# Mixture-of-experts block: results added in memory by the scatter, and a last stage that reads four rows a token

## The reference

```python
    x = layernorm(x + conv_attention(x))
    x = layernorm(x + attention_mlp(x))
    x = layernorm(x + linear_attention(x))
    # 64 experts of width 176, six of them for each token
    topk_w, topk_idx = jax.lax.top_k(softmax(x @ gate_w.T), 6)
    topk_w = topk_w / jnp.sum(topk_w, axis=-1, keepdims=True)
    h = jax.nn.silu(jnp.einsum('th,eih->tei', x, experts_w1))
    y = jnp.einsum('tei,ehi->teh', h, experts_w2)
    routed_out = sum over the six experts e of y[t, e] * topk_w[t, e]
    x = layernorm(x + routed_out + shared_out)
```

## Time and profile before

| | us |
|---|---|
| median of 3 runs | 1036.09 (1034.62 to 1038.6) |
| span of the profiled execution | 1034.5 |
| TensorE busy in it | 967.6 (94%) |
| VectorE busy | 608.1 (59%) |
| GpSimd busy | 456.8 (44%) |
| ScalarE busy | 338.7 (33%) |

### The profile page before, as it was taken

How to read it: one execution, slowest core, us unless ns; L and a number is a source line. 1 busy time by engine, 2 the same in 40 slices (tenths; PEclk the granted TensorE clock), 3 DMA queues, 4 the chain that set the end, 5 groups by cost and what they waited for, 6 DMA issues and landing times. The chain is left out here.

```text
span 1034.5 us, 20988 instructions
## 1 busy us (share of the span) xinstructions
PE 967.6 (94%) x6481; PEld 799.2 (77%) x6481; DVE 608.1 (59%) x2176; ACT 338.7 (33%) x1038; POOL 456.8 (44%) x516
## 2 busy tenths in 40 slices
PE   7988999999999999999999899868999999999986
PEld 6766887877877877877887677647888888888865
DVE  4745466676676676666676546644555555555266
ACT  1244263264264264263263362101111111111243
POOL 1132152283283283283283371541566656656622
PEclk9999999999999999999999999888999999999999
DMA  9597790510510510510510510159869697878296
GB/s 360 192 277 136 203 263 10 133 38 23 137 37 21 137 37 21 137 38 20 128 43 17 129 52 11 64 211 317 335 205 351 211 311 232 295 229 304 85 347 219
DMA packets 103271, 163.28 MB, mean 158 GB/s; under 512 B 26961, under 2 KB 77106, under 8 KB 101042
## 3 DMA queue, kind: packets, MB, share of 16 engines
q1 hardware_dynamic: 85746, 113.31, 37.9%
q0 software_dynamic: 12288, 33.96, 8.7%
q10 hardware_dynamic: 5184, 15.36, 4.1%
HBM read 139.32 MB, written 61.87 MB: 194 GB/s over the span
## 5 line engine op out<-in xcount | busy, mean ns | idle before, releaser
L1282 ACT ACTIVATE prob<-bank,nmx 128x128 f32<-128x128 f32 (+1 forms) x256 | 104.9, 432 | 63.5 <-DVE nmx L1587 63.4
L641 POOL TENSOR_TENSOR prob<-prob,rec 128x512 f32<-128x512 f32 x96 | 99.3, 1041 | 40.8 <-DVE rec L1593 40.0
L673 POOL DMA_INDIRECT x_rows<-x_copy,desti x84 | 85.8, 1021 | 18.3 <-issue 18.3
L1587 DVE TENSOR_REDUCE nmx<-bank 128x2 f32<-128x512 f32 (+1 forms) x96 | 65.1, 685 | 46.6 <-PE bank L889 45.9
L1275 ACT ACTIVATE probT<-bank 128x512 f32<-128x512 f32 x96 | 58.0, 604 | 56.6 <-PE bank L749 55.8
L749 PE MATMUL bank<-cst,prob 128*128 128x128 f32 x384 | 60.6, 282 | 10.3 <-POOL prob L641 6.0
L663 POOL TENSOR_TENSOR products<-z,products 128x512 bf16<-128x512 f32 x8 | 9.2, 1155 | 136.6 <-ACT products L1263 136.6
L949 PE MATMUL bank<-h2T,w_up 128*128 128x256 f32 x256 | 66.4, 382 | 0.0
L951 PE MATMUL bank<-h2T,w_in 128*128 128x256 f32 x256 | 65.7, 379 | 0.0
L749 PEld LDWEIGHTS bank<-cst,prob 128*128 128x128 f32 x384 | 44.4, 145 | 20.2 <-POOL prob L641 10.1
L1282 ACT ACTIVATION_READ_ACCUMULATOR prob<-bank,nmx 128x1 f32 x256 | 55.8, 218 | 0.0
(11 more groups left out here) (445 smaller groups left out, 2500.9 us busy)
## 6 DMA issues: line engine op xcount, KB each, us to landing
w_in<-in_e_w SPq DMA_DIRECT2D x20, 448.0 KB
w_up<-in_e_w SPq DMA_DIRECT2D x20, 448.0 KB
w_down<-in_e_w SPq DMA_DIRECT2D x20, 448.0 KB
products<-in_e_w SPq DMA_DIRECT2D x20, 448.0 KB
prob<-in_e_w SPq DMA_DIRECT2D x20, 448.0 KB
probT<-in_e_w SPq DMA_DIRECT2D x20, 448.0 KB
actT<-in_e_w SPq DMA_DIRECT2D x20, 448.0 KB
x_rows<-sgt SPq DMA_DIRECT2D x1, 8320.0 KB, 28.9
```

Of the source, the lines that this page charges most:

```text
L641: pool.tensor_tensor(p, p, r, ALU.mult).then_inc(S["b_scaled"], 1)
L673: pool.indirect_dma_start(x_rows, bass.IndirectOffsetOnAxis(ap=desti[:, n:n + 1].bitcast(U32), axis=0), rows[:, n // TOPK, :], None).then_ ...
L1282: i = act.activation(prob[:, u % PROBS, h * w:(h + 1) * w], psum(u % 2, h * w, (h + 1) * w), ACT.Exp, bias=nmx[:, u, h:h + 1], accum_out=s ...
L1587: dve.tensor_reduce(nmx[:, u, 0:512 // w], bank[:, u % 2, :].rearrange("p (h k) -> p h k", k=w), AX, ALU.max, negate=True).then_inc(S["b_m ...
```

## The change

- `y_rows` becomes four accumulators: each token has four rows, and chunk n of a quad (n = 0 to 3) adds to row n. The indirect DMA gets `compute_op=ALU.add`. 8704 rows in place of 20608.
- Because an addition needs what is there, SyncE fills `y_rows` with zeros, out of the same `zeros` tile, behind the second fill of `x_rows`; `r_fill` is waited for at 80 in place of 64.
- Each scatter has an `alone` of its own, and waits until the scatter into the same accumulator of the quad before has landed.
- The weights travel with the row: meta data grow from 8 to 14 numbers, `TOPW` goes. `places` finds the weight of the row (`share`), and `result` multiplies by it on the way out of PSUM, four operations of 256 columns in place of two copies of 512.
- In the last turn the weights are worked out per half batch (`E4w`), ahead of `E5p`.
- The last stage loads four rows a token (512 KB) and has eight tiles in flight. TensorE adds them with the plain identity. VectorE adds the residual and takes the statistics; GpSimd does the power and one product; the scaling is an activation on ScalarE, with four output buffers.

```diff
+ACCS = 4
+XW = D + 2 + 2 * TOPK
+Y_ROWS = ACCS * (NB * L + P)
...
-YG = 4
+YG = 8
+OUTS = 4
...
-    c[:, 261:261 + TT] = (np.arange(TT) * P + p[:, None]) * TOPK
+    c[:, 261:261 + TT] = (np.arange(TT) * P + p[:, None]) * ACCS
...
-    blank[:, :, 0] = PAIRS + np.arange((E_N + SPARE + 1) * P).reshape(-1, P)
+    blank[:, :, 0] = ACCS * (NB * L + p)
...
-        outb = [t[:, 0, :] for t in ring(YG, P, 1, D)]
-        yg = [t[:].rearrange("p a b -> p (a b)")[:, 0:TOPK * D].rearrange("p (k d) -> p k d", k=TOPK) for t in (w_in, w_up, actT)]
-        yg.append(products[:].rearrange("p n f d -> p (n f) d")[:, 0:TOPK, :])
-        ON_PE = TOPK - 1
-        diag = [stack[n][:].rearrange("p h k l -> p (h k l)").bitcast(F32)[:, t * ON_PE * P:(t + 1) * ON_PE * P]
-                .rearrange("p (k c) -> p k c", k=ON_PE) for n in "qk" for t in range(2)]
-        ids, choice, found = sb("ids", [P, STREAMS], I32), sb("choice", [P, STREAMS]), sb("found", [P, 4, TOPK])
+        yg = [t[:].rearrange("p a b -> p (a b)")[:, h * ACCS * D:(h + 1) * ACCS * D].rearrange("p (k d) -> p k d", k=ACCS)
+              for h in range(2) for t in (w_in, w_up, w_down, actT)]
+        outb = [stack["k"][:].rearrange("p h k l -> p (h k l)").bitcast(F32)[:, t * D:(t + 1) * D] for t in range(OUTS)]
+        f_rows = stack["q"][:].rearrange("p h k l -> p (h k l)").bitcast(F32)[:, 0:OUTS * D].rearrange("p (t d) -> p t d", t=OUTS)
+        f_st, f_mv = sb("f_st", [P, OUTS, 6]), sb("f_mv", [P, OUTS, 2])
+        f_var, f_root, f_low, f_off = (sb(n, [P, OUTS]) for n in ("f_var", "f_root", "f_low", "f_off"))
+        ids, share, found = sb("ids", [P, STREAMS], I32), sb("share", [P, STREAMS]), sb("found", [P, 4, TOPK])
...
-                "dve": """E2v_0 E2w_0 E3n_0 E2v_1 E3o_0 E2w_1 E3n_1 E4m_0 E3o_1 E4t_0 E4k_0 E4m_1 E5p_0 E4t_1 E4k_1 E5h_0 E5p_1 DTa DTb E5h_1 DTe S0 S1 S2 D4w SD""",
+                "dve": """E2v_0 E2w_0 E3n_0 E2v_1 E3o_0 E2w_1 E3n_1 E4m_0 E3o_1 E4t_0 E4k_0 E4m_1 E4w_0 E5p_0 E4t_1 E4k_1 E4w_1 E5h_0 E5p_1 DTa DTb E5h_1 DTe S0 S1 S2 SD""",
...
             blank(x_rows[E_N * CAP:].rearrange("(n p) d -> p n d", p=P), E_N, SPARE + 1)
+            sp.dma_start(y_rows.rearrange("(n p) d -> p n d", p=P), zeros[:].rearrange("p (o d) -> p o d", o=1).broadcast_to([P, Y_ROWS // P, D])
+                         ).then_inc(S["r_fill"], 16)
             with sp.Fori(2, NB - 1) as b:
                 stack_up(b)
             stack_up(NB - 1)
-            sp.wait_ge(S["r_fill"], 64)
+            sp.wait_ge(S["r_fill"], 80)
...
             def spread(c):
-                need(pool, "p_spare", c.no + NB + 1)
                 pool.wait_ge(S["m_ids"], c.no + 1)
                 late = isinstance(c.no, int) and c.no >= QUADS - 2
                 pool.wait_ge(S["m_y_out"], 2 * c.no + (1 if late else 2))
-                alone(pool)
-                for k in range(4):
+                for k in range(ACCS):
                     if late and k == 2:
                         pool.wait_ge(S["m_y_out"], 2 * c.no + 2)
+                    need(pool, "p_spare", c.no * ACCS + k + NB + 1)
+                    need(pool, f"m_st{k}", c.no * 16)
+                    alone(pool)
                     s, n = 2 * c.slot(2) + k // 2, 4 * c.slot(RING) + k
-                    pool.indirect_dma_start(y_rows, bass.IndirectOffsetOnAxis(ap=ids[:, n:n + 1].bitcast(U32), axis=0), yc[s][:, k % 2, :], None
-                                            ).then_inc(S[f"m_st{s}"], 16)
+                    pool.indirect_dma_start(y_rows, bass.IndirectOffsetOnAxis(ap=ids[:, n:n + 1].bitcast(U32), axis=0), yc[s][:, k % 2, :], None,
+                                            compute_op=ALU.add).then_inc(S[f"m_st{k}"], 16)
             quad_loop(pool, [None, None, spread])
             def root(c):
-                h = c.slot(2)
+                at = slice(c.slot(OUTS), c.slot(OUTS) + 1)
                 pool.wait_ge(S["n_varF"], c.no + 1)
-                pool.tensor_tensor(nrm["F"]["y"][:, h:h + 1], nrm["F"]["v"][:, h:h + 1], minus_half[:, 0:1], ALU.pow
-                                   ).then_inc(S["n_invF"], 1)
+                pool.tensor_tensor(f_root[:, at], f_var[:, at], minus_half[:, 0:1], ALU.pow).then_inc(S["n_invF"], 1)
+                pool.wait_ge(S["n_invF"], c.no + 1)
+                pool.tensor_tensor(f_off[:, at], f_low[:, at], f_root[:, at], ALU.mult).then_inc(S["f_off"], 1)
             tile_loop(pool, [root])
...
                 pe.wait_ge(S[f"f_ld{s}"], c.before(YG) * 16 + 16)
-                pe.wait_ge(S["f_diag"], c.no + 1)
                 need(pe, "f_r", c.no - (YG - 1))
-                for k in range(ON_PE):
-                    mm = pe.matmul(psum(s, 0, D), diag[s][:, k, :], yg[s][:, k, :], start=(k == 0), stop=(k == ON_PE - 1))
+                for k in range(ACCS):
+                    mm = pe.matmul(psum(s, 0, D), ident, yg[s][:, k, :], start=(k == 0), stop=(k == ACCS - 1))
...
                     if n == 0 and first(b):
-                        act.wait_ge(S["r_fill"], 64)
+                        act.wait_ge(S["r_fill"], 80)
                     need(act, "d_sact", b * 3 + n)
...
-                rows = (slice(c.no * P * TOPK, (c.no + 1) * P * TOPK) if isinstance(c.no, int)
-                        else bass.ds(c.no * P * TOPK, P * TOPK))
-                act.dma_start(yg[s], y_rows[rows, :].rearrange("(p k) d -> p k d", k=TOPK)).then_inc(S[f"f_ld{s}"], 16)
-                if not isinstance(c.no, int):
-                    weigh(c)
-            def weigh(c):
-                w = tile_of(TOPW, c.no)
-                for k in range(ON_PE):
-                    i = act.activation(diag[c.slot(YG)][:, k, :], ident, ACT.Identity, scale=w[:, k:k + 1])
-                i.then_inc(S["f_diag"], 1)
+                rows = (slice(c.no * P * ACCS, (c.no + 1) * P * ACCS) if isinstance(c.no, int)
+                        else bass.ds(c.no * P * ACCS, P * ACCS))
+                act.dma_start(yg[s], y_rows[rows, :].rearrange("(p k) d -> p k d", k=ACCS)).then_inc(S[f"f_ld{s}"], 16)
...
             def put(c):
-                h = c.slot(2)
+                h = c.slot(OUTS)
+                at = slice(h, h + 1)
+                act.wait_ge(S["f_off"], c.no + 1)
+                need(act, f"f_st{h}", c.before(OUTS) * 16)
+                act.activation(outb[h], f_rows[:, h, :], ACT.Identity, scale=f_root[:, at], bias=f_off[:, at]).then_inc(S["f_out"], 1)
                 act.wait_ge(S["f_out"], c.no + 1)
                 n = slice(c.no, c.no + 1) if isinstance(c.no, int) else bass.ds(c.no, 1)
                 act.dma_start(out[n].rearrange("o p d -> p (o d)"), outb[h]).then_inc(S[f"f_st{h}"], 16)
-            act.wait_ge(S["d_dest"], NB + TT - 1)
-            for n in range(YG):
-                weigh(Tile(0, n))
-            for s in range(4):
-                act.wait_ge(S[f"m_st{s}"], 32 * (QUADS // 2))
-            tile_loop(act, [collect, None, None, None, put])
-            for h in range(2):
-                act.wait_ge(S[f"f_st{h}"], 16 * (NT // 2))
+            for k in range(ACCS):
+                act.wait_ge(S[f"m_st{k}"], 16 * QUADS)
+            tile_loop(act, [collect, *(YG - 1) * [None], put])
+            for h in range(OUTS):
+                act.wait_ge(S[f"f_st{h}"], 16 * (NT // OUTS))
...
             def D4w(b):
+                need(dve, "d_copied", b)
                 cd.link(dve.tensor_reduce(wsum[:], top8[:, :, 0:TOPK], AX, ALU.add))
                 cd.link(dve.reciprocal(wrec[:], wsum[:]))
-                cd.step(dve.tensor_tensor(slots(TOPW, b), top8[:, :, 0:TOPK],
+                cd.step(dve.tensor_tensor(x3_meta[:, :, 1 + TOPK:1 + 2 * TOPK], top8[:, :, 0:TOPK],
                                           wrec[:].rearrange("p (t o) -> p t o", o=1).broadcast_to([P, TT, TOPK]), ALU.mult))
+            def E4w(tt):
+                def part(b):
+                    need(dve, "d_copied", b)
+                    cd.link(dve.tensor_reduce(wsum[:, tt:tt + 1], top8[:, tt, 0:TOPK], AX, ALU.add))
+                    cd.link(dve.reciprocal(wrec[:, tt:tt + 1], wsum[:, tt:tt + 1]))
+                    cd.step(dve.tensor_scalar(x3_meta[:, tt, 1 + TOPK:1 + 2 * TOPK], top8[:, tt, 0:TOPK], wrec[:, tt:tt + 1], None, ALU.mult))
+                return part
...
-                for j in range(2):
-                    need(dve, f"m_st{2 * c.slot(2) + j}", c.before(2) * 32 - 32)
+                for k in range(ACCS):
+                    need(dve, f"m_st{k}", (c.no - (RING - 1)) * 16)
                 for n in range(4):
                     at, s = 4 * c.no + n, 4 * c.slot(RING) + n
                     meta = xc_row[s][:, D:XW]
                     e = expert_of[:, at:at + 1] if isinstance(c.no, int) else expert_of[:, bass.ds(at, 1)]
-                    i = dve.scalar_tensor_tensor(found[:, n, :], meta[:, 1:1 + TOPK], e, iota[:, 0:TOPK], ALU.is_equal, ALU.mult,
-                                                 accum_out=choice[:, s:s + 1])
```

(50 more changed lines are left out.)

4 lines of the change are left out of this document (2 added, 2 removed).

## The result

| | before | changed |
|---|---|---|
| median of the runs, us | 1035.99 | 1121.86 (1119.78 to 1125.41) |
| span of the profiled execution | 1034.5 | 1123.4 |
| up to the first `S0` | 157.06 | 201.49 |
| from there to the first scatter of results | 560.7 | 560.6 |
| first scatter of results to the landing of the last | 263.2 | 320.7 |

The changed kernel is slower: ratio 1.081, 95% interval 1.078 to 1.0845. The forecast was 1054 with a range of 1038 to 1090. The table accounts for all 88.9 us of span: +44.4 at the start, +57.5 in the expert loop, -13.0 in the last stage, and nothing in between. The profiled execution of the changed kernel took 1125.41 us and is the slowest of the four; the medians are 85.9 us apart.

A forecast was written before the change was run, and what follows sets the result against it. TensorE was taken as busy nearly everywhere, bounding the expert loop at 6.67 us a quad. Span 1034.5 + 25 + 1.5 + 0.3 + 1.3 + 3 - 13 = 1052.6; the median, 1.6 above, gives 1054 us, range 1038 to 1090.

The forecast's parts named there:

- (a): Start: the zero fill of `y_rows` queues ahead of ScalarE's first `sgt` write, landing at 182; +25 us (+15 to +30).
- Rivals C and D: Start: C, new fill runs beside tiny packets, 1038 us, chance 0.09; D, ScalarE's wait isn't reached, 1028 us, chance 0.06.
- (b): After TensorE's stand at the start: a few microseconds at half clock; +1.5 us (0 to 3.5).
- (c): Weights into the rows: +0.3 us (0 to 1); rows of 1080 bytes nothing, up to 1 us where the fill is affected.
- (d): Expert loop: an adding scatter issues on GpSimd in under 1.31 us, hidden under TensorE's 6.67 us a quad.
- rival A: Expert loop: GpSimd becomes the bound, issue 1.44 us, 7.2 us a quad; +21 us, 1075 us, chance 0.18.
- (e): Expert loop: adding reads rows too, between nothing and 1.39 us a quad, mostly absorbed; +3 us (0 to 17).
- (f): Expert loop: four `tensor_scalar` replace two copies on VectorE, +0.3 us a quad, busy 3.52 of 6.67, hidden.
- (g): Last stage: four rows a token and less VectorE work, 40.7 us against 53.6; -13 us (-10 to -14).
- The end of the loop, +1.3 (1 to 4): Last two quads' scatters on GpSimd: 0.3 to 0.4 us more a quad, landing some 0.5 more; +1.3 us.

## Why the prediction was wrong, point by point

- *(a) New fill, +25*: right in mechanism, releaser and size (24.4 us behind the narrow packets, 20 and 24.8 us by the two runs that move it). Where the narrow pieces are mended `S0` lies at 182.56, and the working said 182. Rivals C and D are refuted: the fill landed at 201.4 and all engines stood.
- *(b) Clock, +1.5*: the lower level came as said, but the distance from `S0` to the first scatter is 560.6 us as before. Nothing.
- *(c) Rows of 1080 bytes, "nothing, up to 1 us"*: **wrong by 20 us in the changed kernel's profile, and by 23 in the run with nothing else changed.** I had seen that tiny packets end exactly in time and priced their bytes only. In rows the 260 KB at 34.2 us were 7.8 GB/s, far from a price of bytes, so that what may change with a piece's length and start was the question to put. ScalarE already waited 0.57 us for that DMA, so any delay of it was due in full.
- *(d) Scatter under 1.31 us*: **wrong, the largest miss.** 1.56 us, and behind it 0.39 until the next one. It is rival A, which I gave 0.18 and priced at +21 us with an issue of 1.44; its own formula with 1.56 gives 4 x 1.92 = 7.7 us a quad, +40. Measured were +45 from issue (310.5 against 39.75 x 6.67), +6 of waits between scatters, +4 because the kernel before had issued its last scatters faster than the 6.67 (260.8 in all), and +1.4 from the last landing. The failing step was "I take under 1.31, near the rows": no row showed an adding DMA, and the slack was only 0.35 us a scatter. The argument that plain sizes hardly differ compared 128 rows of 1056 with 128 rows of 1024 bytes, which can't tell a cost for each row from one for the instruction; the run with 64 rows shows that it is mostly the latter, so the conclusion held by luck, and it said nothing of how large that is for another kind. I had also taken the product as 0.34 us ahead of a scatter; beside an adding scatter it takes 0.77 and ends 0.23 us behind it. "Behind that wait only the next scatters are queued" left out VectorE: its `result` waits for landings as well (57.8 us in the 160), and that is the way by which a late scatter holds TensorE.
- *(e) DMA load, +3*: the size of the load was under-rated. It is 2.4 us a quad, not 0 to 1.39. The packets of an adding scatter take 0.94 us of 16 engines against 0.33 for a plain one (48.4% of 160 us for 82, 20.0% for 96), nearly three times, and they are 144 against 48. The Trainium skill ("Collectives: The Full Stack", "The bandwidth ceiling") counts two source reads for the adding step of a collective. In this trace the rows go beyond that rule. The effect on the time stayed small, at most 4 us by the run with fewer transfers, because GpSimd was slower still.
- The estimate of 1.44 us from the Trainium skill ("DMA: Bandwidth & Descriptors", "SWDGE vs HWDGE vs iDMA"), three descriptors a row for two, was nearer than my forecast, but by another mechanism. That section counts a pair of descriptors for each DMA op; taking it for each row was my reading. An additional cost for each row would have halved with 64 rows, and it fell from 0.61 to 0.55.
- *(f) VectorE hidden*: right; with plain scatters the loop is within 1.5 us of before.
- *(g) Last stage, -13*: right, 40.6 against 40.7, tiles 1.9 us apart.
- The end of the loop, +1.3 (1 to 4): under-rated with (d). The landing alone grew by 1.4, and the last quad's four scatters start 1.95 us apart where they started 1.27 apart.

So the terms of the new fill and of the last stage held within a microsecond, and the two for which the trace had no row, a piece of another length and a DMA of another kind, made 77 of the 89 us: 20 at the start and 57 in the loop, where 4 were forecast.

## What to carry to other kernels

Where a resource has a slack of a third of a microsecond an instruction and the change gives it an instruction that the trace doesn't show, don't put the forecast at the nearest row: measure that one instruction first, and count on losses already while it is a little below the threshold. A DMA of thousands of small pieces is priced by piece. What was fast here were 32 bytes starting at multiples of 32 and 64 bytes starting at multiples of 64, also where that meant more bytes (64 bytes 33.7 us, 56 bytes 48.7). A source tile that is shared to save space, and a wait that ends exactly in time, are where a harmless transfer costs its whole length.
